# Every engine's steps in another order, in a kernel that routes tokens through gated attention and experts

## The reference

```python
x = x + tanh(g_xattn[0]) * L0_xattn(layernorm(x), ctx, ctx)        # running sum of ctx*ctx with decay 0.9, times x
x = x + tanh(g_ffn[0]) * L0_ffn(layernorm(x), ...)                 # x @ W.T + the one best of 4 low-rank adapters
x = x + tanh(g_xattn[1]) * L1_xattn(layernorm(x), ctx, ctx, mask)  # 16 heads of 16, probabilities by a sigmoid
x = x + tanh(g_ffn[1]) * L1_ffn(layernorm(x), ...)                 # 8 experts, the best 2 for each token
```

## Time and profile before

| | |
|---|---|
| median of 3 runs | 478.92 us (477.81 to 485.43) |
| the profiled execution, first to last instruction | 478.9 us |
| instructions | 13099 |
| TensorE busy | 396.5 us (83%) |
| VectorE busy | 370.2 us (77%) |
| ScalarE busy | 330.9 us (69%) |
| GpSimd busy | 251.4 us (53%) |
| mean granted TensorE clock | 0.961 of full |

### The profile page before, as it was taken

How to read it: one execution, slowest core, us unless ns; L and a number is a source line. 1 busy time by engine, 2 the same in 40 slices (tenths; PEclk the granted TensorE clock), 3 DMA queues, 4 the chain that set the end, 5 groups by cost and what they waited for, 6 DMA issues and landing times.

```text
span 478.9 us, 13099 instructions
## 1 busy us (share of the span) xinstructions
PE 396.5 (83%) x4092; PEld 309.2 (65%) x4092; DVE 370.2 (77%) x1416; ACT 330.9 (69%) x671; POOL 251.4 (53%) x313
## 2 busy tenths in 40 slices
PE   2758899998999989998899887789568898989950
PEld 1446667776776777676677765478457797777740
DVE  2788888998988889898888785368556566789993
ACT  2755788898889889998888775576616564655640
POOL 1621212545553464637453556678876676766760
PEclk9988999999999999999999999889969999999995
DMA  7336686664575555876454665525353559397975
GB/s 231 90 111 178 181 215 177 183 194 133 166 227 182 162 174 161 244 178 209 144 170 125 220 189 146 166 67 151 90 157 103 165 162 335 101 351 244 330 262 201
DMA packets 69501, 87.12 MB, mean 182 GB/s; under 512 B 9485, under 2 KB 55290, under 8 KB 69306
## 3 DMA queue, kind: packets, MB, share of 16 engines
q1 hardware_dynamic: 60074, 65.81, 47.4%
q0 software_dynamic: 6816, 18.65, 10.5%
q10 hardware_dynamic: 2544, 1.81, 1.2%
HBM read 51.07 MB, written 35.18 MB: 180 GB/s over the span
## 4 chain that ended last, share of the span: by engine, by line
PE 46%; DVE 14%; issue 13%; POOL 11%; ACT 8%; DMA 6%; another core or an unknown queue 1%; ACTq 1%; DVEq 0%; POOLq 0%; SPq 0%
PE ps_J L1654 13%; PE ps_F L1654 6%; PE ps_O L1768 5%; PE ps_T L1663 5%; PE ps_S L1755 4%; POOL store_x L765 4%; POOL pause_t L782 3%; PE ps_S L1654 3%; DMA store_y<-y_out,y_row 2%; POOL store_y L771 2%; PE ps_R L1693 2%; DVE y_out L2938 2%; PE ps_O L1779 2%; PE ps_G L1654 2%; DMA temp_t<-in_temp 2%
## 5 line engine op out<-in xcount | busy, mean ns | idle before, releaser
L771 POOL DMA_INDIRECT store_y<-y_out,y_row x78 | 78.4, 1005 | 41.6 <-DVE y_out L2938 29.5
L765 POOL DMA_INDIRECT store_x<-xn_E,slot_u x64 | 68.8, 1076 | 27.1 <-DVE slot_u L2637 16.9
L1093 ACT ACTIVATE prob<-ps_S 128x512 f32<-128x512 f32 x128 | 72.4, 594 | 12.0 <-PE ps_S L1755 7.6
L1755 PE MATMUL ps_S<-q_stack,k_stack 128*128 128x256 f16 x256 | 44.5, 276 | 5.6 <-issue 3.5
L2926 DVE TENSOR_TENSOR h_lo<-h_f,h_hi 128x512 f16<-128x512 f32 x39 | 26.9, 689 | 24.5 <-ACT h_hi L1177 19.6
L1654 PE MATMUL ps_J<-wout_hi,h_hi 128*128 x112 | 31.2, 278 | 15.2 <-DVE y_out L2938 12.9
L1768 PE MATMUL ps_O<-prob,v_wide 128*32 128x128 f32 x1024 | 41.0, 279 | 1.1 <-ACT prob L1093 0.9
L1169 ACT ACTIVATE h_f<-ps_F,bin_t 128x256 f32<-128x256 f32 x56 | 23.5, 471 | 25.9 <-PE ps_F L1654 20.1
L1654 PE MATMUL ps_F<-xb_hi,win_hi 128*128 128x256 f16 x112 | 31.8, 284 | 4.1 <-DVE xb_lo L2907 2.7
L1779 PE MATMUL ps_O<-wo_t,av 128*128 128x256 f32 x128 | 32.8, 401 | 2.3 <-ACT av L1121 1.6
L751 POOL TENSOR_TENSOR rstd_C<-var_C,minus_half 128x2 f32<-128x2 f32 x16 | 12.2, 761 | 40.3 <-DVE var_C L2416 40.3
(11 more groups left out here) (302 smaller groups left out, 1410.6 us busy)
## 6 DMA issues: line engine op xcount, KB each, us to landing
parts_scratch<-parts SPq DMA_DIRECT2D x32, 256.0 KB
k_stack<-parts_scratch SPq DMA_DIRECT2D x64, 128.0 KB
q_stack<-parts_scratch SPq DMA_DIRECT2D x128, 64.0 KB
xb<-store_x SPq DMA_DIRECT2D x30, 257.0 KB
y_got<-store_y SPq DMA_DIRECT2D x14, 512.0 KB
c_in<-in_ctx SPq DMA_DIRECT2D x16, 256.0 KB
x_in<-in_x SPq DMA_DIRECT2D x16, 256.0 KB
store_x<-zeros SPq DMA_DIRECT2D x15, 257.0 KB, 4.8
```

Of the source, the lines that this page charges most:

```text
L765: pool.indirect_dma_start(store_x, bass.IndirectOffsetOnAxis(slot_u[q][:, at:at + 1], 0), xn_e[q][:, at, :], None).then_inc(s_scat[q], 16)
L771: pool.indirect_dma_start(store_y, bass.IndirectOffsetOnAxis(y_row[n][:, b:b + 1], 0), y_out[n][:, b, :], None).then_inc(s_y_kept[n], 16)
L1093: act.activation(prob[m % PROBS][:, 2 * n:2 * n + 2, :, :], bank_s[n], ACT.Sigmoid, scale=float(HD) ** -0.5).then_inc(s_prob[n], 1)
L1755: ins = pe.matmul(bank_s[n][:, g % 2, :, :], k_stack[q][:, g, k, cut], q_stack[q][:, :, g, k, cut], start=True, stop=True)
```

## The change

All functions stay as they are, and so does every engine's set of calls: 205 on SyncE, 299 on GpSimd, 537 on ScalarE, 637 on TensorE and 1098 on VectorE, counted with the waits between them, with 39 long and 32 short pauses among GpSimd's. The calls are put in another order on every engine, and the loops over tiles are written out. Nearly every region of the lists moves by some places. The parts below are cut from the diff; "..." marks what is left out.

SyncE, the opening:

```diff
+
+
     load_x(0)
+    load_ctx(0)
+    load_x(1)
+    load_ups()
     load_weights(s_wkv, C_K, C_Q)
-    load_x(1)
+    load_ctx(1)
     load_weights(s_wrest, C_Q, WCOLS)
     load_weights(s_wbase, C_BASE, C_K)
-    load_ctx(1)
-    load_ups()
     load_matrix(0)
     load_ctx(2)
+    load_constants()
     load_x(2)
-    load_constants()
-    load_matrix(1)
-    load_x(3)
-    load_projection()
-    load_ctx(3)
...
     sp.wait_ge(s_zero, 4)
     zero_first(0)
     zero_first(1)
+    zero_spare(0)
+    load_matrix(1)
     zero_first(2)
-    stack_keys(2)
+    keep_parts("k", 0)
```

GpSimd, from pair 11's last scatters to tile 12. From there to tile 38 the short pauses stand in groups of one to three at some tiles and are absent at others:

```diff
     scatter(12, 3)
     long_pause()
+    long_pause()
+    long_pause()
     scatter(12, 1)
-    long_pause()
     scatter(12, 2)
-    long_pause()
     scatter(12, 0)
     inverse_root("E", 14)
+    long_pause()
+    long_pause()
+    long_pause()
+    long_pause()
+    long_pause()
+    long_pause()
+    long_pause()
     scatter(13, 3)
     long_pause()
     scatter(13, 0)
-    long_pause()
     scatter(13, 1)
     long_pause()
     scatter(13, 2)
-    long_pause()
     scatter(14, 3)
-    long_pause()
-    scatter(14, 2)
-    long_pause()
-    scatter(14, 1)
-    long_pause()
-    scatter(14, 0)
     inverse_root("E", 15)
     keep_block(0, 0)
-    long_pause()
     keep_block(0, 1)
-    long_pause()
     keep_block(1, 0)
-    long_pause()
+    scatter(14, 2)
     keep_block(1, 1)
-    long_pause()
     keep_block(2, 0)
-    long_pause()
     keep_block(2, 1)
-    long_pause()
+    scatter(14, 1)
+    keep_block(3, 0)
+    keep_block(3, 1)
+    pause()
+    scatter(14, 0)
     scatter(15, 3)
-    long_pause()
+    pause()
     scatter(15, 0)
-    long_pause()
+    keep_block(4, 0)
+    keep_block(4, 1)
+    keep_block(5, 0)
+    keep_block(5, 1)
+    keep_block(6, 0)
+    keep_block(6, 1)
+    keep_block(7, 0)
+    pause()
+    keep_block(7, 1)
+    keep_block(8, 0)
+    keep_block(8, 1)
+    keep_block(9, 0)
     scatter(15, 1)
-    long_pause()
     scatter(15, 2)
-    long_pause()
-    keep_block(3, 0)
-    long_pause()
-    keep_block(3, 1)
-
-    for i in range(4, TILES):
-        keep_block(i, 0)
-        if i < CLOSE:
-            pause()
-        keep_block(i, 1)
+    keep_block(9, 1)
+    keep_block(10, 0)
+    keep_block(10, 1)
+    pause()
```

ScalarE, the opening and the end (of its eight first loads, `decay_t` moves behind `gates_raw` and `temp_t`):

```diff
+    hi_ctx(0)
+    squared(0)
     gates_tanh()
-    squared(0)
     gained(0)
+    gained(1)
     squared(1)
-    hi_ctx(0)
     temperature_exp()
-    matrix_hi(0)
+    identity_half()
+    ups_hi()
...
     keep_pair(ON_SP)
-    for n in range(TAIL, NP):
-        copy_x3(n)
-    for n in range(ON_SP + 1, NP - 1):
-        keep_pair(n)
-    for b in range(2):
-        keep_batch(NP - 1, b)
+    keep_pair(11)
+    copy_x3(13)
+    copy_x3(14)
+    copy_x3(15)
+    keep_pair(13)
+    keep_pair(12)
+    keep_pair(14)
+    keep_batch(15, 0)
+    keep_batch(15, 1)
```

TensorE, the tiles:

```diff
-    for i in range(7, TILES + 2):
-        if i < TILES:
-            transpose_block(i)
-        if i - 1 < TILES:
-            for m in range(KT):
-                layer1(i - 1, m)
-        for b in range(SUB):
-            layer2(i - 2, b)
+    layer1(6, 0)
+    layer1(6, 1)
+    transpose_block(8)
+    layer2(5, 0)
+    layer2(5, 1)
+    layer1(7, 0)
+    layer1(7, 1)
+    layer2(6, 0)
...
+    layer2(13, 0)
+    layer2(13, 1)
+    transpose_block(16)
+    transpose_block(17)
+    layer1(15, 0)
+    layer1(15, 1)
+    layer2(14, 0)
+    layer2(14, 1)
```

VectorE, tiles 7 to 14, and the end:

```diff
     copy_lo(7)
-    next(final)
-    take_rows(7)
-    next(final)
-    next(final)
-    hidden_lo(6)
-    next(final)
-    add_bias(5)
-    next(final)
+    router_diff(15)
+    add_bias(4)
+    hidden_lo(5)
+    slots(15)
     next(final)
     copy_lo(8)
     next(final)
     next(final)
-    take_rows(8)
+    take_rows(7)
     next(final)
-    next(final)
+    add_bias(5)
+    hidden_lo(6)
     hidden_lo(7)
-    next(final)
     add_bias(6)
     copy_lo(9)
     next(final)
+    hidden_lo(8)
+    add_bias(7)
+    take_rows(8)
+    copy_lo(10)
     next(final)
-    take_rows(9)
+    next(final)
+    hidden_lo(9)
+    add_bias(8)
+    copy_lo(11)
     next(final)
     next(final)
     next(final)
-    hidden_lo(8)
-    add_bias(7)
     next(final)
     next(final)
-    copy_lo(10)
+    next(final)
+    next(final)
+    take_rows(9)
+    add_bias(9)
+    next(final)
+    next(final)
+    hidden_lo(10)
+    copy_lo(12)
+    next(final)
     next(final)
     take_rows(10)
+    copy_lo(13)
+    hidden_lo(11)
+    add_bias(10)
     next(final)
-    hidden_lo(9)
-    add_bias(8)
-
-    for i in range(11, TILES + 2):
-        if i < TILES:
-            copy_lo(i)
-            take_rows(i)
-        if i - 1 < TILES:
-            hidden_lo(i - 1)
-        add_bias(i - 2)
-        if EARLY + 4 <= i < EARLY + 12:
-            next(gates)
-        if ADD_AT <= i <= TILES:
-            add_pair(i - ADD_AT)
-
-
-    for n in range(TILES + 1 - ADD_AT, NP):
-        add_pair(n)
+    take_rows(11)
+    add_bias(11)
+    hidden_lo(12)
...
+    take_rows(36)
+    take_rows(37)
+    add_bias(36)
+    add_pair(9)
+    take_rows(38)
+    add_bias(37)
+    hidden_lo(38)
+    add_bias(38)
+    add_pair(10)
+    add_pair(11)
+    add_pair(12)
+    add_pair(13)
+    add_pair(14)
```

More of the change, by code:

```diff
@@ L3043, in _ @@
             part_lo("k", 0)
+            means("A", 2)
             adapter_logits(0)
+            variances("A", 2)
             adapter_max(0)
             adapter_diff(0)
-            moves(1)
-            statistics_a(2)
             make_x1(1)
@@ L3915, in _ @@
             router_max(15)
-            take_rows(5)
+            hidden_lo(4)
             router_index(15)
@@ new lines, in _ @@
+            add_bias(11)
+            hidden_lo(12)
+            copy_lo(14)
+            take_rows(12)
+            add_bias(12)
+            hidden_lo(13)
+            copy_lo(15)
+            next(gates)
+            hidden_lo(14)
+            take_rows(13)
+            add_bias(13)
+            copy_lo(16)
+            take_rows(14)
+            next(gates)
+            copy_lo(17)
+            hidden_lo(15)
+            add_bias(14)
+            take_rows(15)
+            take_rows(16)
+            hidden_lo(16)
@@ new lines, in _ @@
+            take_rows(17)
+            add_bias(15)
+            copy_lo(18)
+            hidden_lo(17)
+            take_rows(18)
+            copy_lo(19)
+            take_rows(19)
+            add_bias(16)
+            next(gates)
+            add_bias(17)
+            hidden_lo(18)
+            copy_lo(20)
+            take_rows(20)
+            next(gates)
+            hidden_lo(19)
+            copy_lo(21)
+            add_bias(18)
+            hidden_lo(20)
+            copy_lo(22)
+            add_bias(19)
@@ new lines, in _ @@
+            next(gates)
+            take_rows(21)
+            take_rows(22)
+            hidden_lo(21)
+            copy_lo(23)
+            take_rows(23)
+            next(gates)
+            next(gates)
+            add_bias(20)
+            hidden_lo(22)
+            copy_lo(24)
+            add_bias(21)
+            add_bias(22)
+            hidden_lo(23)
+            take_rows(24)
+            next(gates)
+            copy_lo(25)
+            hidden_lo(24)
+            copy_lo(26)
+            add_bias(23)
@@ new lines, in _ @@
+            hidden_lo(25)
+            copy_lo(27)
+            take_rows(25)
+            take_rows(26)
+            add_bias(24)
+            add_bias(25)
+            hidden_lo(26)
+            take_rows(27)
+            copy_lo(28)
+            copy_lo(29)
+            take_rows(28)
+            add_bias(26)
+            hidden_lo(27)
+            add_pair(0)
+            add_pair(1)
+            hidden_lo(28)
+            add_bias(27)
+            copy_lo(30)
+            copy_lo(31)
+            add_bias(28)
@@ new lines, in _ @@
+            hidden_lo(29)
+            add_pair(2)
+            add_pair(3)
+            take_rows(29)
+            hidden_lo(30)
+            add_bias(29)
+            copy_lo(32)
+            copy_lo(33)
+            add_pair(4)
+            hidden_lo(31)
+            take_rows(30)
+            add_bias(30)
+            copy_lo(34)
+            hidden_lo(32)
+            take_rows(31)
+            add_bias(31)
+            add_pair(5)
+            hidden_lo(33)
+            copy_lo(35)
+            add_pair(6)
```

1931 lines of the change are left out of this document (1168 added, 763 removed).

## The result

Over 20 runs of each the changed kernel took 483.85 us in the median and the kernel before 481.21 us. The ratio is 1.0072 with a 95% interval of 1.0046 to 1.0098: it is slower by 0.7%, and the forecast was 462 us, 3.5% faster.

The account below looks back on a forecast made before the run. Bounds taken: TensorE in the pair stage, GpSimd's queue in the changeover, signals held by close scatters in the middle, VectorE at the end. Terms -1.5 - 1 - 2 - 8 + 0 - 2 - 2.5 = -17: 478.9 to 462 us, range 452 to 477.

Parts of the forecast that it names:

- Opening, pairs, changeover until add_bias(5): Three terms for the stretches up to add_bias(5): opening -1.5 us, pair stage -1 us, changeover -2 us.
- the cover I had named: Changeover: seven pauses ahead of scatter(13, 3) cost nothing if GpSimd waits there for slots(13); otherwise 6.8 us.
- The ring stall: VectorE's 6.04 us wait at take_rows(8) for the five output buffers goes: -10.9 us, 3 given back, net -8.
- nine tiles with 27 close scatters: From keep_block(0, 0) to (9, 1), scatters 1.35 us apart take 36.5 us, giving back up to 4.3 us; 3 taken.
- signals are held: Claim that GpSimd's close scatters delay TensorE's signals to ScalarE and VectorE, 2.59 us in the case read.
- The clock of 1.00: Sign of being right: granted clock 1.00 near add_bias(6), where its mean from 321.9 to 360 us was 0.87.
- Load of tile 16 on: load_block(16) waits for later VectorE steps and scatters but just fits: 0, bounds 0 and +6 us.
- Middle tiles: Pauses at chosen tiles only; 17 tiles lose 0.51 us each, 8.7 in all, a quarter recovered: -2 us.
- The gelu of the earlier trace: A middle-tile gelu started at 397.92 us, its matmul ended at 395.33, ScalarE idle; read as held by close scatters.
- Last tiles: Two of twelve pairs' adds go behind add_bias(38), 3.1 us off a full VectorE: -2.5 us.
- The stall goes, the rest doesn't come: Rival, chance 0.23: -8 from the ring, 4 given back by pauses or late loads, end and middle -2: 473 us.
- the slower one: Rival, chance 0.10: close scatters hold TensorE's signals in nine tiles, 2.59 us a tile, 23.3 in all: 490 us.

Follow-up runs that it names:

- e1: Changed order up to add_bias(9) on every engine, order of the kernel before behind it, one short pause between a tile's scatters: 457.0 us beside 467.0, ratio 0.977.
- e18: e1 unaltered, run a third time, on a chip where signals are held: 482.4 us, ratio to the kernel before 0.985.
- e3: Changed kernel with one alteration on GpSimd: from tile 10 one short pause between each tile's two scatters to 35, as before; ratio to the kernel before 0.998.
- e6: Changed order up to add_bias(9), order of before to add_bias(26), changed order again behind it; ratio to the kernel before 1.012.
- e7: e1 without any short pause from tile 10 on: 484.4 us, ratio to the kernel before 0.990.
- e12: e1 unaltered, run again beside e9 on one chip: 460.76 us, ratio to the kernel before 0.983.
- e13: Changed kernel with hidden_lo(38) moved ahead of add_bias(37) on VectorE; ratio to the kernel before 1.000.
- e17: e1 with a long pause between a tile's two scatters from tile 10 to 27, short from 28 to 35: 474.9 us, ratio to the kernel before 0.977.
- e9: e1 with long pauses between a tile's scatters from tile 6 to 27 and behind scatter(15, 1) and (15, 2): 466.75 us, ratio to before 0.995.

## Why the prediction was wrong

**Opening, pairs, changeover until add_bias(5), -4.5 together: not there.** TensorE's wait of 3.48 us fell to 1.68, and another of 2.48 us came, ending at 60.76. slots(0) comes 2.8 us later than before, so no gain of the opening is seen there. The first tile is 3.5 us earlier, but the last pair isn't. VectorE's slots(15) in the changed kernel and in the one before:

```profile
336.53 0.18 DVE L3043 TENSOR_REDUCE slot_u<-pick_row 128x4 uint32<-128x32 f32 x1
```

```profile
333.09 0.18 DVE L2637 TENSOR_REDUCE slot_u<-pick_row 128x4 uint32<-128x32 f32 x1
```

Tile work seems to have been put in front of pair work, not added to idle time. The seven pauses ahead of scatter(13, 3) cost nothing: GpSimd waited for slots(13) behind them, the cover I had named.

```profile
299.67 5.29 POOL L842 TENSOR_TENSOR pause_t<-half_ones,minus_half 128x2 f32<-128x2 f32 x7
308.16 1.04 POOL L825 DMA_INDIRECT store_x<-xn_E,slot_u  x1 [3.20 <-DVE slot_u L3043]
```

**The ring stall, -8: right.** It gave 6.9 us in the trace and 9.5 in e1. That nine tiles with 27 close scatters give some back is shown where signals are held (e18 has 16.7 us for the four tiles, e1 14.3), not elsewhere. The clock of 1.00 that I named as a sign wasn't there: it was 0.76 from 345 to 352 us.

**Load of tile 16 on, 0: right**; no such wait is in the trace.

**Middle tiles, -2 with bounds of -8.7 and +4: the first step that failed, with the wrong sign.** It was +5.1. I costed only where the pauses go. Steps in twos were in the lists (transpose_block(12) and (13), copy_hi and copy_lo likewise), and I put no price on them: TensorE waits 1.63 and 1.71 us at the first place, in the second wait ScalarE's table load of 1.28 us, and the changed order costs 3.4 us over the middle where nothing is held (e3 against e1). What held signals added in this very trace can be told only in part: xb_hi starts over 1 us late with ScalarE idle at 375.83, 391.04, 408.10 and 411.15 us, but e3, where nothing was held, has such starts too (1.4 us, at the transposes in twos). The gelu at 417.22, 3.48 us late, with TensorE's stop of 2.50 us and the lower clock behind it, has nothing like it in e3. The kernel before has late starts of its own, up to 2.55 us, but no such stop, and so the 5.1 us stay undivided. e18's middle is 14 us longer than e1's, the same file; how much of that is due to held signals alone is not shown. The gelu of the earlier trace rows was read rightly, but the effect behind it is not in every job.

**Last tiles, -2.5 with bounds of -4.5 and 0: the second step that failed.** It was +4.8, and 4.8 to 6.9 in every pair of traces. I took 2 x 1.57 us of adds off "a full VectorE" and ruled out a loss without a reason. A full engine's order decides who waits for it: hidden_lo feeds TensorE at once, an add feeds nobody for a long time, and the change put adds and add_bias ahead of hidden_lo. That such an order loses is shown by e6 (1.012, where the same front with the old last tiles had 0.990 in its own job, e7, and 0.977 to 0.985 in e1, e12 and e18). Through which waits it does so in the changed kernel is argued: 2.5 of the 4.8 us lie at hidden_lo(38) behind add_bias(37), with the clock at 0.50 behind that stop, but moving that one call (e13) left the whole time where it was, and the other 2.3 us lie in waits under 1 us that no run takes apart.

None of the rivals was this one. "The stall goes, the rest doesn't come" had the right shape and stopped 11 us short; the slower one had its price in the wrong nine tiles.

**A version that beats both.** Changed order up to tile 9, old loops behind (e1): 0.977, 0.983 and 0.985. With long pauses from tile 10 to 27 (e17) 0.977 where signals are held; where they aren't, it was not run, and e9, which is near it, took 6 us more than e1's order beside it (e12).
